# Linear attention inside a four-part network: prefix sums by scans along tokens, or by triangular matmuls with the token on the partition

## The chip, the cores and the metric

The kernel runs on one core of a Trainium2 chip. The metric is the device time of one execution in microseconds (us), taken as the median over runs. Before the change it is 2098.7 us (3 runs, 2096.18 to 2099.93). Everything is float32 in and out.

## What is computed

The input is 4 batches of 1024 tokens with 128 features. Four blocks follow each other, each with a layer norm and a residual: softmax attention, a top-2 mixture of 32 experts, linear attention, and the experts again. Only the linear attention is touched. It has 16 heads of 8 features; for each head:

```
qf = softplus(x @ Wq.T) * (sigmoid(x @ Wg.T + bg) + 1e-6)
kf = softplus(x @ Wk.T)
v  = x @ Wv.T
kv_cum = cumsum over tokens of kf[d] * v[e]        # 8 x 8 running sums
z_cum  = cumsum over tokens of kf[d]               # 8 running sums
num[e] = sum over d of qf[d] * kv_cum[d, e]
den    = sum over d of qf[d] * z_cum[d] + 1e-6
out    = (num / den) @ Wo.T
```

The running sums start again with each batch.

## The kernel before, in words

`network` runs the parts one after the other, each in a block of its own that ends with a barrier of all engines: load, `normalise`, `attention`, `normalise`, `experts`, `normalise`, `linear_attention` (L1096 to L1493), `normalise`, `experts`, `store`. `normalise` leaves the normalised input transposed, features on partitions, as a high part `k.xT_hi` and a rest `k.xT_lo`; a product in this split form takes three matmuls (`three`, L1416).

`linear_attention` works on 8 groups of 512 tokens. A tile has 128 partitions (16 heads times 8 features d) by 512 tokens; the second feature index e is unrolled into 8 columns, and column 0 stands for the denominator. For each group:

- TensorE makes gate, query and key (`projections`) and, for each e, v[e] spread over the d of its head (`v_column`, three matmuls each).
- ScalarE forms the gate and the logarithm of softplus (three table loads) and copies every second v column out of PSUM.
- The products k times v are split: odd e on VectorE (`kv`, L1334), even e on GpSimd (L1240).
- VectorE takes the running sum over the 512 tokens (`scan`, L1348), nine for each group, and does softplus, the reciprocal and the adding to x.
- GpSimd multiplies the nine running sums with the query (`product`, L1252).
- TensorE sums over d with a matrix of ones (`sum_over_d`, L1447 and L1452), then applies Wo (L1468).

Each engine has a hand-written order (`slot`) in which three groups overlap: `s` is projected, `s - 1` is summed, `s - 2` is finished. Counting semaphores tie the engines together; `pipeline` runs the middle slots in a loop over batches, where waits go through a register (`Rounds`), and SyncE fetches the input of each group into `xs_hi` and `xs_lo`. PSUM holds `z` (3 banks), `v_ps` (2), `num` (2) and `den_y` (1).

Of the kernel before, what the change touches and what calls it, by code (L numbers as in the profile page):

```python
# [7 lines left out]
ALU = mybir.AluOpType  # L8
# [1087 lines left out]
def linear_attention(nc, k, wq_dram, wk_dram, wv_dram, wo_dram, wg_dram, bg_dram):  # L1096

    HEADS, DH = 16, 8
    GATE_EPS, DEN_EPS = 1e-6, 1e-6
    HALVES = N // GT
    ROUNDS = B
    LEAD = 2
    COLS = DH + 1
    RING = 4  # L1110
    WEIGHTS = 5
    WQ, WK, WG, WV, WO = range(WEIGHTS)
    ZQ, ZK, ZG = (slice(n * GT, (n + 1) * GT) for n in range(3))

    SUM_ORDER = [1, 2, 3, 0, 4, 5, 6, 7, 8]
    SUM_AT = {j: n for n, j in enumerate(SUM_ORDER)}

    with ExitStack() as stack:
        s_ = Scope(nc, stack, "linear")
        sb, ps, sem = s_.sb, s_.ps, s_.sem  # L1120
        two = range(2)
        w = sb("w", [P, WEIGHTS, D])
        wT_hi, wT_lo = sb("wT_hi", [P, 3, D], F32R), sb("wT_lo", [P, 3, D], F32R)

        wv_hi, wv_lo = sb("wv_hi", [P, DH, HEADS, DH], F32R), sb("wv_lo", [P, DH, HEADS, DH], F32R)
        woT = sb("woT", [P, D])
        bg, ones = sb("bg", [P, 1]), sb("ones", [P, GT])
        same_head = sb("same_head", [P, HEADS, DH])
        into = sb("into", [P, DH, HEADS, DH])
        xs_hi = [sb(f"xs_hi{i}", [P, GT], F32R) for i in two]  # L1130
        xs_lo = [sb(f"xs_lo{i}", [P, GT], F32R) for i in two]
        log = sb("log", [P, 2 * GT])
        gate, soft_q = sb("gate", [P, GT]), sb("soft_q", [P, GT])
        q, kk = ([sb(f"{n}{i}", [P, GT]) for i in two] for n in ("q", "k"))
        v_col = [sb(f"v_col{i}", [P, GT]) for i in two]
        kv_dve, kv_pool = ([sb(f"{n}{i}", [P, GT]) for i in two] for n in ("kv_dve", "kv_pool"))
        cum = [[sb(f"cum{i}_{j}", [P, GT]) for j in range(COLS)] for i in two]
        prod0 = [sb(f"prod0_{i}", [P, GT]) for i in two]
        prod = [sb(f"prod{i}", [P, GT]) for i in range(RING)]
        den_inv, oT = ([sb(f"{n}{i}", [P, GT]) for i in two] for n in ("den_inv", "oT"))  # L1140
        z = ps("z", (P, 3 * GT))
        v_ps = [ps(f"v_ps{i}") for i in two]
        num = [ps(f"num{i}") for i in two]
        den_y = ps("den_y")

        w_in, bg_in, turned_ok, hi_ok, wT_ok, cleared, same_ok, const_ok = (sem(n) for n in (
            "w_in", "bg_in", "turned_ok", "hi_ok", "wT_ok", "cleared", "same_ok", "const_ok"))
        xs_in = [sem(f"xs_in{i}") for i in two]
        (z_ok, v_ok, v_out, kv_dve_ok, kv_pool_ok, cum_ok, prod_ok, sum_ok, gate_ok, log_step, soft_ok, q_ok,
         den_step, oT_ok, y_ok, x_ok) = (sem(n) for n in (  # L1150
             "z_ok", "v_ok", "v_out", "kv_dve_ok", "kv_pool_ok", "cum_ok", "prod_ok", "sum_ok", "gate_ok", "log_step",
             "soft_ok", "q_ok", "den_step", "oT_ok", "y_ok", "x_ok"))
        PER = {id(x): n * HALVES for x, n in (
            (z_ok, 1), (v_ok, DH), (v_out, 4), (kv_dve_ok, 4), (kv_pool_ok, 4), (cum_ok, COLS), (prod_ok, COLS),
            (sum_ok, COLS), (gate_ok, 1), (log_step, 3), (soft_ok, 2), (q_ok, 1), (den_step, 2), (oT_ok, 1), (y_ok, 1), (x_ok, 1))}

        def rounds(engine, *sems):
            scratch = engine.alloc_register(f"linear_value_{engine.engine.name}")
            return [Rounds(engine, x, PER[id(x)], scratch) for x in sems]

        def at(r, g, n=0):

            m = g * (r.per // HALVES) + n
            r.now(m) if m >= 0 else r.before(m + r.per)
# [395 lines left out]
```

## Time and profile before

| what | value |
|---|---|
| median of the runs | 2098.7 us |
| the profiled execution | 2101.55 us, its span 2099.6 us |
| TensorE busy | 1835.9 us (87%) |
| VectorE busy | 1683.0 us (80%) |
| GpSimd busy | 1346.3 us (64%) |
| ScalarE busy | 956.1 us (46%) |
| linear-attention stage | from 1590.2 to 1854.9 us of the span |
| mean granted TensorE clock, whole span | 0.941 |

The parts run one after the other, so an engine's share of the whole span is a mean over stages with different limits; the stage in question is read by itself. A granted clock of 1.0 is TensorE's 2.4 GHz, 0.5 its 1.2 GHz. The profiled execution took 2.9 us more than the median.

### The profile page before, as it was taken

To read this page: it belongs to the slowest core of one execution; us is meant where nothing else is said; L and a number is where in the kernel's file an instruction comes from. 1 tells how busy PE (TensorE), PEld (TensorE's weight loads), DVE (VectorE), ACT (ScalarE), POOL (GpSimd) and SP (SyncE) were. 2 spreads that over 40 slices of the span, in tenths; PEclk is the share of its full clock that TensorE was granted. 3 is DMA by queue.
4 is the path that set the end of the run, shared out by engine and by line. 5 is a ranking of instruction groups with operands and counts; after the bars stand their busy time and mean duration, and the time that the engine had idled before them with its cause. 6 is when DMAs were issued, how large, how long until landed. Compare 5 with 4: busy or idle time off the path is not lost. (4 is left out here: it accounts for less than half of the span.)

```text
span 2099.6 us, 35185 instructions
## 1 busy us (share of the span) xinstructions
PE 1835.9 (87%) x11743; PEld 1283.3 (61%) x11743; DVE 1683.0 (80%) x2683; ACT 956.1 (46%) x1920; POOL 1346.3 (64%) x1156
## 2 busy tenths in 40 slices
PE   2999999999999999999999998579974776666997
PEld 1666766666666666676666665458853333345885
DVE  4888888888888888888888886678874887967886
ACT  3344444444444444444444443347864323234885
POOL 2467657657667667667667668169972766714997
PEclk9999999999999999999999999589985989957998
DMA  2000000000000000000000000100000000000001
GB/s 81 1 1 1 2 1 1 1 1 2 1 1 1 1 1 1 1 1 1 1 1 1 2 1 1 41 31 21 30 0 26 21 20 19 2 1 31 21 30 40
DMA packets 22102, 23.20 MB, mean 11 GB/s; under 512 B 1296, under 2 KB 15440, under 8 KB 21968
## 3 DMA queue, kind: packets, MB, share of 16 engines
q1 hardware_dynamic: 21968, 21.40, 3.1%
q8 instruction: 85, 1.39, 0.3%
q14 instruction: 49, 0.40, 0.1%
HBM read 6.72 MB, written 2.10 MB: 4 GB/s over the span
## 5 line engine op out<-in xcount | busy, mean ns | idle before, releaser
L866 DVE TENSOR_REDUCE attn_neg<-attn_shared 128x2 f32<-128x1024 f32 x512 | 618.3, 1225 | 172.9 <-PE attn_shared L990 171.5
L806 ACT ACTIVATE attn_prob<-attn_shared 128x1024 f32<-128x1024 f32 (+3 forms) x384 | 311.0, 812 | 411.2 <-PE attn_shared L1018 411.2
L768 POOL TENSOR_TENSOR attn_row_sum<-attn_row_sum,attn_prob 128x1024 f32<-128x1024 f32 (+3 forms) x256 | 418.7, 1636 | 24.2
L481 ACT ACTIVATE experts_weighed<-experts_y,experts_gate 128x128 f32<-128x128 f32 x1024 | 278.1, 382 | 112.0 <-PE experts_y L570 108.6
L508 DVE SCALAR_TENSOR_TENSOR experts_acc<-experts_y,experts_gate,experts_acc 128x128 f32<-128x128 f32 x960 | 268.6, 344 | 43.4 <-PE experts_y L570 33.2
L763 POOL TENSOR_TENSOR attn_row_sum<-attn_prob 128x1024 f32<-128x1024 f32 x64 | 135.5, 2118 | 222.6 <-ACT attn_prob L806 220.1
L1035 PE MATMUL attn_pv<-attn_prob,attn_v 128*64 128x512 f32 (+3 forms) x1536 | 267.5, 490 | 1.2 <-POOL attn_prob L745 1.2
L568 PE MATMUL experts_y<-kept_w_hi,experts_xs_hi 128*128 128x512 f32 x512 | 201.2, 393 | 45.2 <-DMA experts_xs_lo<-kept_xT_lo 45.2
L986 PE MATMUL attn_shared<-attn_qk_hi 64*128 64x512 f32 x1024 | 223.0, 424 | 4.1 <-DVE attn_qk_lo L884 2.4
L890 DVE RECIPROCAL attn_den<-attn_den 128x256 f32<-128x256 f32 x128 | 214.6, 1718 | 12.1 <-ACT attn_den L829 12.1
L745 POOL TENSOR_TENSOR attn_prob<-attn_prob,attn_below 128x256 f32<-128x256 f32 x256 | 187.4, 732 | 49.6 <-ACT attn_prob L806 45.6
L990 PE MATMUL attn_shared<-attn_qk_hi,attn_qk_lo 64*128 64x512 f32 x1024 | 208.5, 392 | 0.0
L988 PE MATMUL attn_shared<-attn_qk_lo,attn_qk_hi 64*128 64x512 f32 x1024 | 207.6, 391 | 0.0
L1035 PEld LDWEIGHTS attn_pv<-attn_prob,attn_v 128*64 128x64 f32 x1536 | 104.4, 137 | 162.7 <-issue 148.8
L569 PE MATMUL experts_y<-kept_w_lo,experts_xs_hi 128*128 128x512 f32 x512 | 200.7, 392 | 0.0
L570 PE MATMUL experts_y<-kept_w_hi,experts_xs_lo 128*128 128x512 f32 x512 | 200.6, 392 | 0.0
L449 POOL TENSOR_TENSOR experts_quad_sum<-experts_quad_sum,experts_weighed 128x512 f32<-128x512 f32 x128 | 168.1, 1332 | 11.7 <-ACT experts_weighed L481 11.2
L775 POOL TENSOR_TENSOR attn_o_norm<-attn_o,attn_den 128x512 f32<-128x512 f32 x64 | 82.0, 1283 | 132.9 <-DVE attn_den L890 132.9
L986 PEld LDWEIGHTS attn_shared<-attn_qk_hi 64*128 64x128 f32 x1024 | 101.8, 184 | 90.7 <-issue 58.0
L1012 PE MATMUL attn_shared<-attn_qk_hi 64*128 64x512 f32 (+3 forms) x768 | 147.2, 374 | 9.8 <-DVE attn_neg L866 5.0
L1452 PE MATMUL linear_num<-linear_prod,linear_into 128*128 128x512 f32 x128 | 83.7, 748 | 67.7 <-POOL linear_prod L1252 67.6
L568 PEld LDWEIGHTS experts_y<-kept_w_hi,experts_xs_hi 128*128 128x128 f32 x512 | 97.2, 190 | 65.8 <-issue 45.4
(192 smaller groups left out, 3558.2 us busy)
## 6 DMA issues: line engine op xcount, KB each, us to landing
experts_xs_hi<-kept_xT_hi SPq DMA_DIRECT2D x16, 256.0 KB, 2.3
experts_xs_lo<-kept_xT_lo SPq DMA_DIRECT2D x16, 256.0 KB, 2.4
kept_x<-in_L_attn_a_x_dram SPq DMA_DIRECT2D x4, 512.0 KB, 6.2
norm_f_w_raw<-_ffn_expert_weights_dram SPq DMA_DIRECT2D x4, 512.0 KB, 6.1
linear_xs_hi<-kept_xT_hi SPq DMA_DIRECT2D x8, 256.0 KB, 2.3
linear_xs_lo<-kept_xT_lo SPq DMA_DIRECT2D x8, 256.0 KB, 2.4
out_dram<-kept_x SPq DMA_DIRECT2D x4, 512.0 KB, 5.4
attn_prob<-in_L_attn_a_Wkv_dram SPq DMA_DIRECT2D x2, 512.0 KB, 5.5
```

The source lines that it names most:

```text
L481: ins = act.activation(weighed[n][:, e, :], y[(2 * quad + odd) % BANKS][:, e * D:(e + 1) * D], ACT.Copy, scale=g)
L508: dve.scalar_tensor_tensor(out=acc[i][:, c, :], in0=y[(2 * quad + odd) % BANKS][:, e * D:(e + 1) * D], scalar=gate[i][:, c, quad * PER + e ...
L568: pe.matmul(out, xs_hi[i][:, at], hi, start=True, stop=False)
L569: pe.matmul(out, xs_hi[i][:, at], lo, start=False, stop=False)
L768: pool.tensor_tensor(row_sum[n][:, :, at:], row_sum[n][:, :, at:], src[:, :, at:], ALU.add).then_inc(add_ok, 1)
L806: act.activation(prob[n % RING][:, :, at:], buffer((p, i))[:, :, at:], ACT.Exp).then_inc(exp_ok, 1)
L866: dve.tensor_reduce(neg[p % 2][:, :, b, half], buffer((p, b, half))[:, :, :], AX.X, ALU.max, negate=True).then_inc(max_ok, 1)
L890: dve.reciprocal(den[n][:, at], den[n][:, at]).then_inc(inv_ok, 1)
L986: pe.matmul(buffer(u)[:, h, :], hi[head(h), 0, rows], hi[head(h), 1, at], start=True, stop=False)
L988: pe.matmul(buffer(u)[:, h, :], hi[head(h), 0, rows], lo[head(h), 1, at], start=False, stop=False)
L990: ins = pe.matmul(buffer(u)[:, h, :], lo[head(h), 0, rows], hi[head(h), 1, at], start=False, stop=True)
L1035: ins = pe.matmul(pv[head(h), first:], v[g % 2][:, j, cols], prob[(UNITS * p + i) % RING][:, h, first:], start=(j == 0), stop=(i in (7, 11)))
```

## The change

`linear_attention` is written anew; nothing else differs. Tokens now lie on the partitions, 128 (a chunk) at a time, four chunks to a group, 32 in all. The feature index d is innermost in memory.

- `project` makes gate, query, key and v of one chunk in one bank `z` of 512 columns: three matmuls of 512 columns, and one of 128 that adds the bias. ScalarE copies it out as `raw` (384 columns) and `v` (128, written into slots of nine, the ninth holds 1).
- `curves` (ScalarE) forms sigmoid and the logarithm of softplus for a whole group; `soften` (VectorE) ends softplus, `queries` (GpSimd) makes q.
- `outer` (GpSimd): the product k[d] times v[e], nine e by 128 columns: 1152 elements a chunk, into one of three `kv` buffers.
- `within` (TensorE): a matmul with the triangular matrix `upto` sums over the tokens of the chunk up to each, 3 pieces of 384 columns, into `cum` (3 banks, two of these).
- `carried` (TensorE): what the earlier chunks give, q transposed times `state`, 3 pieces of 48 columns, written into the ninth slot of each head. `add_state` keeps the sum over tokens in `state_ps`, and `new_state` (VectorE) masks it to each head's own.
- `weigh` (VectorE) multiplies the 1296 sums of a chunk with `q1` (q with a ninth slot that holds 1), and `add_up` sums nine neighbours. Then `floor` (ScalarE), `invert` (VectorE, 64 elements), `divide` (GpSimd), `turn_o` and `out` (TensorE), `into_x` (VectorE).
- `turn_q` transposes q for `carried`. `turn_q`, `project`, `turn_o` and `out` all use the one bank `z` in turn, and ScalarE or VectorE empties it each time.
- The eight groups are written out without a loop (`STEPS` is 11), and TensorE reads `k.xT_hi` and `k.xT_lo` in place; SyncE fetches only weights.

The core of the diff, with the order of ScalarE and VectorE:

```diff
+            def outer(g, c):
+                n = g * GROUP + c
+                pool.wait_ge(soft_ok, g + 1)
+                pool.wait_ge(v_ok, n + 1)
+                if n >= KV_RING:
+                    pool.wait_ge(cum_ok, n - KV_RING + 1)
+                pool.tensor_tensor(kv[n % KV_RING][:, :, :, :],
+                                   key(g, c).rearrange("p (h d) -> p h d", d=DH).unsqueeze(1).to_broadcast([P, E1, HEADS, DH]),
+                                   v[g % 3][:, c, :, :].rearrange("p h e -> p e h").unsqueeze(3).to_broadcast([P, E1, HEADS, DH]),
+                                   ALU.mult).then_inc(kv_ok, 1)
...
+                pool.tensor_tensor(o[:, :, :, :], num[g % 2][:, :, 0:DH, :].rearrange("p c e h -> p c h e"),
+                                   inv[:, :, :].unsqueeze(3).to_broadcast([P, GROUP, HEADS, DH]), ALU.mult).then_inc(o_ok, 1)
+
+            for s in range(STEPS):
+                g = s - 2
+                if exists(g):
+                    outer(g, 0)
+                    outer(g, 1)
+                if exists(g - 1):
+                    divide(g - 1)
+                if exists(g):
+                    outer(g, 2)
+                if exists(s - 1):
+                    queries(s - 1)
+                if exists(g):
+                    outer(g, 3)
...
+            def curves(g):
+                act.wait_ge(raw_ok, GROUP * (g + 1))
+                if g:
+                    act.wait_ge(soft_ok, g)
+                    act.wait_ge(q_ok, g)
...
+            def widen(g):
+                act.wait_ge(q_ok, g + 1)
...
+            for s in range(STEPS):
+                g = s - 2
+                if exists(g):
+                    q_out(g)
+                    widen(g)
+                if exists(s):
+                    projected(s, 0)
+                if exists(g - 1):
+                    floor(g - 1)
+                if exists(s):
+                    for c in range(1, GROUP):
+                        projected(s, c)
+                if exists(g - 1):
+                    o_out(g - 1)
+                if exists(s):
+                    curves(s)
...
-                    start = cum[0][j][:, GT - 1:GT] if i else 0.0
-                    dve.tensor_tensor_scan(cum[i][j][:, :], ones[:, :], src[:, :], start,
-                                           ALU.mult, ALU.add).then_inc(cum_ok, 1)
...
+            for s in range(STEPS):
+                g = s - 2
+                for c in range(GROUP):
+                    if exists(g):
+                        n = g * GROUP + c
+                        weigh(g, c)
+                        if not begins(n + 1):
+                            new_state(n + 1)
+                        add_up(g, c)
+                    if c == 0 and exists(g - 1):
+                        invert(g - 1)
+                    if c == 1 and exists(s - 1):
+                        soften(s - 1)
+                    if c == 2 and exists(g - 1):
+                        into_x(g - 1)
...
+            def within(g, c):
+                n = g * GROUP + c
+                pe.wait_ge(kv_ok, n + 1)
+                if n >= 2:
+                    pe.wait_ge(prod_ok, n - 1)
```

How the order moves, first on ScalarE in a middle slot. Before, the gate, the logarithm's steps and the copies of v columns are interleaved:

```order
L333 REGISTER_ALU [waits linear_z_ok]
L1295 ACTIVATE linear_gate<-linear_z,linear_bg 128x512 [waits linear_q_ok]
L333 REGISTER_ALU [waits linear_v_ok]
L1289 ACTIVATE linear_v_col<-linear_v_ps 128x512 [waits linear_kv_pool_ok]
L1299 ACTIVATE linear_log<-linear_z 128x1024 [waits linear_soft_ok]
L1301 ACTIVATE linear_log<-linear_log 128x1024 [waits linear_log_step]
```

After, from the end of one step (`linear_oT` is the copy of `turn_o`) into the next (`linear_qT` is the copy of `turn_q`):

```order
L1284 ACTIVATE linear_oT<-linear_z 128x512 [waits linear_o_turned]
L1257 ACT_TABLE_LOAD [waits linear_q_ok,linear_soft_ok]
L1257 ACTIVATE linear_gate<-linear_raw 128x512 [waits linear_raw_ok]
L1259 ACTIVATE linear_gate<-linear_gate 128x512 [waits linear_gate_step]
L1260 ACTIVATE linear_log<-linear_raw 128x1024
L1262 ACTIVATE linear_log<-linear_log 128x1024 [waits linear_log_step]
L1264 ACTIVATE linear_log<-linear_log,linear_upto 128x1024 [waits linear_log_step]
L1274 ACTIVATE linear_qT<-linear_z 128x512 [waits linear_q_turned]
L1270 ACTIVATE linear_q_1<-linear_q 128x64x8 [waits linear_prod_ok,linear_q_ok]
L1245 ACTIVATE linear_raw<-linear_z 128x384 [waits linear_soft_ok,linear_z_ok]
```

The whole of `curves` stands in one piece between the last copy of a step and the first of the next. Two of its three table loads are not printed in this form.

On TensorE, before, around the sum for the denominator:

```order
L1452 MATMUL linear_num<-linear_prod,linear_into 128x512
L333 REGISTER_ALU x2
L1447 MATMUL linear_den_y<-linear_prod_1,linear_same_head 128x512
L333 REGISTER_ALU
L1417 MATMUL linear_v_ps<-linear_xs_hi,linear_wv_hi 128x512
L1418 MATMUL linear_v_ps<-linear_xs_lo,linear_wv_hi 128x512
L1419 MATMUL linear_v_ps<-linear_xs_hi,linear_wv_lo 128x512
```

After, from the third chunk of a group into the next step:

```order
L1415 MATMUL linear_cum<-linear_kv,linear_upto 128x48x8 x3
L1398 MATMUL linear_z<-kept_ident,linear_o 128x128 x4
L1426 MATMUL linear_cum<-linear_state,linear_qT 128x48 x3
L1435 MATMUL linear_state_ps<-linear_v,linear_soft 128x144
L1405 MATMUL linear_z<-linear_woT,linear_oT 128x128 x4
L1415 MATMUL linear_cum<-linear_kv,linear_upto 128x48x8 x3
L1426 MATMUL linear_cum<-linear_state,linear_qT 128x48 x3
L1435 MATMUL linear_state_ps<-linear_v,linear_soft 128x144
L1392 MATMUL linear_z<-kept_ident,linear_q 128x128 x4
L1415 MATMUL linear_cum<-linear_kv,linear_upto 128x48x8 x3
L1384 MATMUL linear_z<-linear_wT_hi,kept_xT_hi 128x512
```

`turn_o` (L1398) now stands behind `within` of the third chunk, and `project` (L1384) of the next group behind the transposes of q (L1392), whose copy it waits for.

## Rows read from the trace of the kernel before

**Rows 1.** Windows, the stage: us; busy PE, PEld, DVE, ACT, POOL; PEclk; DMA, GB/s.
```profile
1590.20:1854.90 264.70, 174.18 (x477) 96.22 (x477) 201.45 (x162) 81.15 (x91) 167.88 (x117) 0.84 0.05 17
```
**Rows 2.** Timeline, first projection and last operation of the stage: start us, us, engine.
```profile
1599.50 0.76 PE L1417 MATMUL linear_z<-linear_xs_hi,linear_wT_hi 128*128 128x512 f32 x1 [4.30 <-DVE linear_wv_lo L1318]
...
1854.19 0.69 DVE L1369 TENSOR_TENSOR kept_x<-linear_den_y,kept_x 128x512 f32<-128x512 f32 x1 [1.25 <-PE linear_den_y L1468]
```
**Rows 3.** Waits of the stage: who waits, for whom; us in total, times, longest.
```profile
PE linear_num L1452 <- POOL linear_prod L1252: 67.6, 35, 4.5
...
DVE linear_den_inv L1377 <- PE linear_den_y L1447: 21.4, 7, 5.0
```
**Rows 4.** Timeline, VectorE's reciprocals of two neighbouring groups.
```profile
1729.76 3.32 DVE L1398 RECIPROCAL linear_den_inv<-linear_den_inv 128x512 f32<-128x512 f32 x1
...
1760.60 3.32 DVE L1398 RECIPROCAL linear_den_inv<-linear_den_inv 128x512 f32<-128x512 f32 x1
```
**Rows 5.** Groups by shape, VectorE (count, busy us, mean ns of one).
```profile
L866 DVE TENSOR_REDUCE attn_neg<-attn_shared 128x2 f32<-128x1024 f32 x512 | 618.3, 1225 | 172.9 <-PE attn_shared L990 171.5
...
L890 DVE RECIPROCAL attn_den<-attn_den 128x256 f32<-128x256 f32 x128 | 214.6, 1718 | 12.1 <-ACT attn_den L829 12.1
...
L884 DVE TENSOR_TENSOR attn_qk_lo<-attn_shared,attn_qk_hi 128x1024 fp32r<-128x1024 f32 x64 | 73.7, 1189 | 7.7 <-POOL kept_x L738 7.0 <-ACT attn_qk_hi L810 0.7
...
L1348 DVE TENSOR_TENSOR_SCAN linear_cum<-linear_ones,linear_cum,linear_kv_pool 128x512 f32<-128x512 f32 x16 | 28.2, 1761 | 1.1 <-POOL linear_kv_pool L1240 1.1
...
L1398 DVE RECIPROCAL linear_den_inv<-linear_den_inv 128x512 f32<-128x512 f32 x8 | 26.6, 3321 | 0.0
...
L1334 DVE TENSOR_TENSOR linear_kv_dve<-linear_v_ps,linear_k 128x512 f32<-128x512 f32 x32 | 21.3, 667 | 19.7 <-PE linear_v_ps L1419 19.4
...
L1393 DVE SCALAR_TENSOR_TENSOR linear_q<-linear_gate,linear_soft_q 128x512 f32<-128x512 f32 x8 | 13.0, 1629 | 0.1
```
**Rows 6.** Groups by shape, GpSimd.
```profile
L768 POOL TENSOR_TENSOR attn_row_sum<-attn_row_sum,attn_prob 128x1024 f32<-128x1024 f32 x96 | 229.3, 2388 | 11.7
...
L1252 POOL TENSOR_TENSOR linear_prod<-linear_q,linear_cum 128x512 f32<-128x512 f32 x72 | 116.8, 1641 | 24.1 <-DVE linear_cum L1348 21.6 <-PE linear_num L1452 2.5
...
L768 POOL TENSOR_TENSOR attn_row_sum<-attn_row_sum,attn_prob 128x512 f32<-128x512 f32 x64 | 82.5, 1289 | 5.0
```
**Rows 7.** Groups by shape, ScalarE.
```profile
L806 ACT ACTIVATE attn_prob<-attn_shared 128x256 f32<-128x256 f32 x64 | 24.6, 385 | 46.1 <-PE attn_shared L1018 46.1
...
L1289 ACT ACTIVATE linear_v_col<-linear_v_ps 128x512 f32<-128x512 f32 x32 | 19.0, 595 | 119.2 <-PE linear_v_ps L1419 119.2
...
L1301 ACT ACT_TABLE_LOAD x8 | 10.3, 1283 | 0.1
...
L1305 ACT ACTIVATE linear_log<-linear_log,linear_ones 128x1024 f32<-128x1024 f32 x8 | 9.2, 1149 | 0.1
...
L1301 ACT ACTIVATE linear_log<-linear_log 128x1024 f32<-128x1024 f32 x8 | 8.5, 1057 | 0.1
...
L1295 ACT ACTIVATE linear_gate<-linear_z,linear_bg 128x512 f32<-128x512 f32 x8 | 5.5, 687 | 7.3 <-PE linear_z L1419 7.3
```
**Rows 8.** Timeline, TensorE matmuls in the middle of the stage.
```profile
1727.14 2.08 PE L1452 MATMUL linear_num<-linear_prod,linear_into 128*128 128x512 f32 x2 [2.38 <-POOL linear_prod L1252]
...
1734.09 0.40 PE L1418 MATMUL linear_z<-linear_xs_lo,linear_wT_hi 128*128 128x512 f32 x1
...
1734.32 0.39 PE L1419 MATMUL linear_z<-linear_xs_hi,linear_wT_lo 128*128 128x512 f32 x1
...
1737.66 1.15 PE L1468 MATMUL linear_den_y<-linear_woT,linear_oT 128*128 128x128 f32 x8 [0.85 <-DVE linear_oT L1360]
...
1742.02 1.12 PE L1452 MATMUL linear_num<-linear_prod,linear_into 128*128 128x512 f32 x2 [2.51 <-POOL linear_prod L1252]
...
1748.58 2.07 PE L1452 MATMUL linear_num<-linear_prod,linear_into 128*128 128x512 f32 x2 [3.18 <-POOL linear_prod L1252]
```
**Rows 9.** Granted clock, one stretch of the stage, columns as in rows 1.
```profile
1749.00:1753.00 4.00, 4.00 (x6) 1.73 (x6) 0.52 (x1) 0.00 (x0) 0.74 (x1) 0.50 0.00 0
```

More of the change, by code:

```diff
@@ L1128, in linear_attention @@
[L1128 to L1147, printed above, removed]
@@ L1184, in exists @@
-        def exists(g, r):
-            return g >= 0 and not (isinstance(r, int) and r == ROUNDS - 1 and g >= HALVES)
-        block = s_.block()
+        bg_raw, bg = sb("bg_raw", [P, D]), sb("bg", [P, D], F32R)
+        pick_raw, pick = sb("pick_raw", [P, P]), sb("pick", [P, P], F32R)
+        upto, own = sb("upto", [P, P]), sb("own", [P, HEADS])
+        raw = [sb(f"raw{i}", [P, GROUP, 3 * D]) for i in two]
+        v = [sb(f"v{i}", [P, GROUP, HEADS, E1]) for i in three]
+        log = sb("log", [P, GROUP, 2 * D])
@@ new lines, in invert, with into_x, soften @@
+            def invert(g):
+                dve.wait_ge(den_ok, g + 1)
+                if g:
+                    dve.wait_ge(o_ok, g)
+                dve.reciprocal(inv[:, :, :], den[:, :, :]).then_inc(inv_ok, 1)
+            def into_x(g):
+                x = k.x[:, g * GROUP:(g + 1) * GROUP, :]
+                dve.wait_ge(y_ok, g + 1)
+                dve.tensor_tensor(x, z[:, :].rearrange("p (c d) -> p c d", d=D), x, ALU.add).then_inc(x_ok, 1)
+            def soften(g):
+                dve.wait_ge(log_step, 3 * (g + 1))
+                if g >= 2:
+                    dve.wait_ge(kv_ok, GROUP * (g - 1))
+                    dve.wait_ge(q_ok, g - 1)
+                    dve.wait_ge(added_ok, updates(GROUP * (g - 1)))
+                dve.scalar_tensor_tensor(out=soft[g % 2][:, :, :], in0=raw[g % 2][:, :, D:3 * D], scalar=0.0, in1=log[:, :, :],
+                                         op0=ALU.max, op1=ALU.add).then_inc(soft_ok, 1)
@@ new lines, in turn_q, with turn_o @@
+            def turn_q(g):
+                pe.wait_ge(q_ok, g + 1)
+                for c in range(GROUP):
+                    ins = pe.transpose(z[:, c * P:(c + 1) * P], q[:, c, :], k.ident[:, :])
+                ins.then_inc(q_turned, 1)
+            def turn_o(g):
+                pe.wait_ge(o_ok, g + 1)
+                for c in range(GROUP):
+                    ins = pe.transpose(z[:, c * P:(c + 1) * P], o[:, c, :, :].rearrange("p h e -> p (h e)"), k.ident[:, :])
+                ins.then_inc(o_turned, 1)
@@ new lines, in carried @@
+            def carried(g, c):
+                n = g * GROUP + c
+                m = updates(n)
+                pe.wait_ge(qT_ok, g + 1)
+                if not begins(n):
+                    pe.wait_ge(state_ok, m)
+                held = empty if begins(n) else state[m % 2]
+                for b in range(3):
+                    to = sums(n)[:, b, :, :].rearrange("p e (h d) -> p e h d", d=E1)[:, :, :, DH]
+                    ins = pe.matmul(to, qT[g % 2][:, c * P:(c + 1) * P], held[:, 3 * b:3 * b + 3, :], start=True, stop=True)
+                ins.then_inc(cum_ok, 1)
```

520 lines of the change are left out of this document (218 added, 302 removed).

## The prediction

> **What bounds the kernel now.** The parts of the network run one after the other with a barrier between them, and the diff touches only the linear attention, so I read that stage alone. First the windows view over 1590.2 to 1854.9 us [rows 1]: in 264.7 us VectorE is busy 201.5, TensorE 174.2, GpSimd 167.9 and ScalarE 81.2, and the granted clock is 0.84. No engine is full: the stage is a ring of waits. The waits view [rows 3] shows two links: TensorE waits 67.6 us for GpSimd's products, and VectorE 21.4 us for the denominator that TensorE sums from them, 5.0 us at the longest. The timeline [rows 4] gives the period: reciprocals of neighbouring groups start at 1729.76 and 1760.60, so a group costs 30.8 us. Of this VectorE works 201.5 / 8 = 25.2 us [rows 1], mostly nine scans of about 1.76 us and a reciprocal of 3.32 [rows 5]. So the old limit is VectorE's work plus one round trip over GpSimd and TensorE, eight times, and a start: 9.3 us pass up to the first projection [rows 2].
>
> **What is removed.** For each group nine scans (15.8 us), the reciprocal over 512 columns (3.32) and four products of k and v on VectorE (2.7) [rows 5]; nine products and four of k and v on GpSimd, thirteen operations of 512 columns, 21 us by 167.9 / 8 [rows 1]; 24 matmuls for v columns on TensorE. Also the eight fetches of xs from the resident input: no wait for them is among the rows, I cost them at nothing.
>
> **What is added, engine by engine and group.** I price by width, along rows of the same kind.
>
> - VectorE: an operation with one operand in PSUM takes 0.667 us for 512 columns and 1.189 for 1024 [rows 5], so 1.02 ns a column: `weigh` (1296) 1.47, `new_state` (144) 0.29. A reduction takes 1.225 for 1024, so `add_up` (1296) 1.50. The reciprocal is 1.718 for 256 and 3.321 for 512, so 64 columns cost 0.52. `soften` is 1.19 undisturbed, 3.3 if it suffers like the query product (1.629 for 512). `into_x` 0.67. Sum 4 x 3.26 + 0.52 + 1.19 + 0.67 = 15.4 us.
> - GpSimd: 1.289 for 512 columns, 2.388 for 1024 [rows 6], so `outer` (1152) is 2.66; four of them, `queries` and `divide` at 1.29 each: 13.2 us.
> - ScalarE [rows 7]: `curves` is three table loads (3.85), sigmoid 0.69, its copy 0.60, absolute value and exponential 1.06 each, logarithm 1.15, together 8.4. Copies: 0.60 for 512, 0.385 for 256, so 0.49 and 0.28 for `raw` and `v`. With `q_out`, `widen`, `o_out` and `floor`: 13.6 us.
> - TensorE at full clock [rows 8]: a matmul of the split form and 512 columns starts 0.23 us after the last (1734.09, 1734.32) and ends 0.17 later than it would stream. A plain float32 product is two instructions: 1.12 for the pair at 512 columns, 0.17 of it the end, so about 0.92, and 384 columns cost 0.69. Eight instructions of 128 columns take 1.15, so 0.12 each. So: `project` 0.82, `within` 3 x 0.69 = 2.07, `carried` six short instructions 0.73, `add_state` 0.27, `turn_q` and `turn_o` 0.5 each, `out` 0.98. Sum 4 x 3.89 + 2.0 = 17.5 us. I have no row for a transpose at full clock and took 0.12; at 0.24 each a turn is 1.0.
>
> No engine reaches 20 us, against 30.8. What decides is the ring.
>
> **The new ring.** `curves` of group s stands in one piece on ScalarE ahead of `q_out` of the next step, as the order rows show, and all projections queue on bank z behind `q_out`. Following the waits through one step:
>
> `curves` 8.4; `q_out` 0.6; `project` and `carried` of the first chunk 0.82 + 0.73 + 0.17; `weigh` 1.47; `new_state` 0.29; `add_up` 1.50; `invert` 0.52 (it stands behind `add_up`); `divide` 1.29; third `outer` 2.66 (behind `divide` on GpSimd); third `within` 2.07; `turn_o` with its end 0.67 (behind that `within`); `o_out` 0.6; then `curves` again. Sum 21.8 us. The handovers (about 0.06 each) are paid for by operations of VectorE and ScalarE that start before the last has ended.
>
> Beside it lies this: `soften` follows the second `add_up`, `queries` and the fourth `outer` follow `soften`; the last `add_up` comes out some 2 us ahead of the `floor` that needs it. That cover of 2 us is all: if the third `outer` holds `soften` back for longer, this branch ends last. The second `within` and projections 2 to 4 fill TensorE's waits.
>
> The ring holds 4.1 us of TensorE at full clock. Here the clock does not stay full: after 2.38 us idle the pair took 2.08, after 2.51 us 1.12, after 3.18 us 2.07 [rows 8], and such a stretch shows 0.50 in the windows [rows 9]. The new step has idle times of about 1.7 and 2.3 us, so some of them may be followed by half clock. I take the stage's mean of 0.84: 4.1 / 0.84 = 4.9, and the step is 22.6 us.
>
> **Two readings of GpSimd.** On the same 512 columns GpSimd took 1.641 in the old stage and 1.289 in the attention [rows 6], and VectorE's scan 1.76. Of the new operations of VectorE only `soften` has both tensors in SBUF, so I price GpSimd undisturbed. At 1641 / 1289 = 1.27 for all, `outer` would be 3.39 and `divide` 1.64, the step 1.1 us longer, the total 7 to 8 us more. The Trainium skill, SBUF — State Buffer, Who interferes with whom, says that a VectorE instruction with two SBUF inputs contends with a GpSimd instruction that reads SBUF and that one with a single SBUF input does not. The trace agrees as far as rows go: 1.641 beside the scans, 1.289 without. By the rule the sum is the one that I use.
>
> **The whole stage.** Lead: 9.3 us less the two 1024-wide splits of v's weights (about 2.2) is 7.1 to the first `project`. Then four chunks at half clock, each `project` 1.7, ends 0.2, copies 0.77: 10.4. `curves` of group 0, 8.4. Four chunks of group 1, the first projected already: 8.6. `curves` of group 1, 8.4. That is 42.9 us in which nothing overlaps. Then six steps with a `curves` in the ring: 6 x 22.6 = 135.6. Group 6 has no projections: about 20 us to its last `add_up`; group 7 about 18; its finish (`floor` 0.3, `invert` 0.52, `divide` 1.29, `turn_o` 0.67, copy 0.6, `out` 1.15, `into_x` 0.67) 5.2; with 1.5 for the clock 45. Sum 223.5 us against 264.7, a gain of 41.2. Against the profiled execution, 2101.6 us, that gives 2060.4; this lies 2.9 us above the median shown, so against 2098.7 the forecast is 2057.5, in round figures 2058. The median is told from no change beyond about 0.2%, 4.2 us.
>
> **Rivals.**
>
> - *GpSimd's strided reads cost more.* `outer` repeats v across eight neighbours and walks it with a step of nine elements; `divide` reads `num` with a step of 16. All of rows 6 run over neighbours, so no row speaks for or against it. At the dearest pace among them, 1.641 us for 512 or 3.2 ns a column, `outer` is 3.7 and `divide` 1.64: the ring grows by 1.0 + 0.35 to 24.0, while GpSimd's own 17.7 us stay below it. `soften` waits longer behind the third `outer`, and the branch with the fourth closes in. With 1.4 us over six steps, 3 over the last two and some 3 for that branch it is 2072. The Trainium skill, GPSIMD Engine Reference, Performance pitfalls for Q7 kernels, gives about 50% more for reads with a step above 8 bytes; by it, as an estimate, `outer` would be 4.0 and the total about 2076; no run here shows it yet. Chance 0.24.
> - *TensorE stays at half clock (the other side).* At 0.5 the group needs 35 us of TensorE, more than the old period, and the loop becomes TensorE's own queue: 36 us a step with what cannot be filled. From 1.2 GHz throughout: 43 + 6 x 36 + 80 = 339 us, 74 more than now, 2173. The turning point is where 43 + 6 T + 45 = 264.7, a step of 29.4 us. For it: stretches at 0.50 exist [rows 9]. Against: they follow idle times of 2.4 us and more in a stage where TensorE is busy for 66% of it [rows 1]; here 17.5 / 22.6 = 77%. Only a clock near half all the time, or half clock with the dearer GpSimd, passes the point. Chance 0.10.
> - *The ring does not close as I drew it.* If `curves` is cheaper or the clock stays full, the step is 21 to 21.8 and the total 2042 to 2052. Chance 0.14, counted as its own below 2046.
> - *The change does not do what it says.* The v columns and scans are gone from the order rows, so the work has changed; a stage that comes out equal by chance: 0.02.
>
> **How the numbers follow.** My own case (2046 to 2066) has 0.50, dearer GpSimd 0.24, cheaper 0.14, half clock 0.10, equal 0.02. The predicted time is that of the likeliest, 2058. The range takes in the clock at full (2042, and 4 below for narrow operations that I may price too high) and dearer GpSimd with `soften` at 3.3 and the clock at 0.75 (2072 + 14): 2038 to 2086, which leaves out the slow end. Faster by over 0.2%: 0.88; within: 0.02; slower: 0.10.
>
> **What would show it.** Right: the stage is about 223 us; `inv` reciprocals of neighbouring groups lie 22 to 23 us apart; ScalarE's idle time before `linear_oT` ends on TensorE; the third `within` waits for GpSimd; GpSimd's 1152-wide product near 2.7 us; VectorE's 1296-wide pair near 1.5 each. Wrong: `outer` at 4 us; TensorE's granted clock below 0.75 over the stage; VectorE without idle time; or a step above 25 us.

## The result, and the profile after

The changed kernel takes 2066.5 us (median of 4 runs, 2065.55 to 2068.0) against 2099.3 beside it: a ratio of 0.984, 95% interval 0.983 to 0.986. The gain is 32.8 us, where 41.2 were forecast (2058). The profiled execution has a span of 2064.6 us. Outside the linear attention nothing moved: it begins at 1589.9 (before: 1590.2), and from its end to the end of the span there are 245 us in both traces.

Windows view of the changed kernel. Columns: stretch, its us; busy us of PE, PEld, DVE, ACT, POOL; PEclk; DMA share, GB/s. First the stage, then its lead (the time up to the first step) and the six steps that have a `curves` in them; the end, 49.7 us, is not printed. A step runs from one `linear_qT` copy of ScalarE to the next.

```profile
1589.90:1819.40 229.50, 169.56 (x701) 121.55 (x701) 118.47 (x119) 102.84 (x164) 97.23 (x61) 0.80 0.01 2
...
1589.90:1631.10 41.20, 20.23 (x47) 12.84 (x47) 2.48 (x4) 22.98 (x37) 10.18 (x16) 0.54 0.03 8
1631.10:1655.30 24.20, 19.46 (x71) 14.72 (x72) 11.43 (x11) 11.97 (x19) 8.25 (x4) 0.72 0.00 1
1655.30:1677.70 22.40, 18.66 (x93) 13.36 (x91) 16.74 (x17) 12.65 (x20) 11.94 (x6) 1.00 0.00 1
1677.70:1699.10 21.40, 17.29 (x88) 12.77 (x88) 14.72 (x15) 12.69 (x22) 11.92 (x6) 1.00 0.00 0
1699.10:1722.10 23.00, 18.59 (x86) 13.27 (x86) 14.60 (x14) 12.60 (x21) 11.92 (x6) 0.93 0.00 1
1722.10:1746.30 24.20, 20.80 (x86) 15.49 (x87) 12.99 (x14) 12.66 (x22) 11.91 (x6) 0.79 0.00 1
1746.30:1769.40 23.10, 19.35 (x90) 13.83 (x88) 16.23 (x17) 12.62 (x21) 11.95 (x6) 0.93 0.01 1
```

Read this against [rows 1]: 229.5 us instead of 264.7, VectorE busy 118.5 instead of 201.5, GpSimd 97.2 instead of 167.9, TensorE 169.6 against 174.2. That is the whole gain of about 35 us in the trace (span 2099.6 to 2064.6). The period, 30.8 us before [rows 4], is 21.4 us where the granted clock is 1.00 throughout, and 24.2 where it is 0.79 and 0.72. The step of 22.4 us ran at 1.00 as well, but began with a leftover of the slow one before it: the last `within` of that step ended at 1657.25, 1.9 us after the copy of q had begun, and held back the first projection.

Groups by shape of the changed kernel (count, busy us, mean ns of one, idle time before them):

```profile
L1324 DVE TENSOR_TENSOR linear_prod<-linear_cum,linear_q 128x1296 f32<-128x1296 f32 x32 | 48.2, 1506 | 81.2 <-PE linear_cum L1426 81.1
L1333 DVE TENSOR_REDUCE linear_num<-linear_prod 128x144 f32<-128x1296 f32 x32 | 47.8, 1494 | 0.1
L1352 DVE SCALAR_TENSOR_TENSOR linear_soft<-linear_raw,linear_log 128x1024 f32<-128x1024 f32 x8 | 9.7, 1217 | 18.6 <-ACT linear_log L1264 18.6
L1339 DVE RECIPROCAL linear_inv<-linear_den 128x64 f32<-128x64 f32 x8 | 4.4, 545 | 0.3 <-ACT linear_den L1280 0.3
...
L1194 POOL TENSOR_TENSOR linear_kv<-linear_soft,linear_v 128x1152 f32<-128x1152 f32 x32 | 75.3, 2374 | 0.0
L1212 POOL TENSOR_TENSOR linear_o<-linear_num,linear_inv 128x512 f32<-128x512 f32 x8 | 10.6, 1320 | 70.5 <-DVE linear_inv L1339 70.5
```

These answer to [rows 5, 6]: no scan, no wide reciprocal; the pair of 1296 costs 1.51 and 1.49 us, the outer product 2.37.

Waits of the changed kernel's stage (who, for whom: us in all, times, longest):

```profile
DVE linear_prod L1324 <- PE linear_cum L1426: 81.1, 25, 18.8
...
ACT linear_oT L1284 <- PE linear_z L1398: 48.8, 8, 12.8
...
PE linear_cum L1415 <- POOL linear_kv L1194: 22.6, 10, 4.3
```

TensorE waits 22.6 us for GpSimd, where it waited 67.6 [rows 3]; VectorE now waits 81.1 us and ScalarE 48.8 for TensorE. The ring closes as drawn: `divide` at 1683.80, the third outer behind it, TensorE behind that, `oT` behind `turn_o`, then the next table load. Timeline of the changed kernel in the step with full clock (start us, us, engine; the projections and the other chunks left out):

```profile
1683.80 1.32 POOL L1212 TENSOR_TENSOR linear_o<-linear_num,linear_inv 128x512 f32<-128x512 f32 x1 [7.87 <-DVE linear_inv L1339]
...
1685.08 2.37 POOL L1194 TENSOR_TENSOR linear_kv<-linear_soft,linear_v 128x1152 f32<-128x1152 f32 x1
...
1687.51 2.20 PE L1415 MATMUL linear_cum<-linear_kv,linear_upto 128*128 128x384 f32 x6 [1.85 <-POOL linear_kv L1194]
...
1689.04 1.26 POOL L1205 TENSOR_TENSOR linear_q<-linear_gate,linear_soft 128x512 f32<-128x512 f32 x1 [1.59 <-issue]
...
1690.18 0.60 ACT L1284 ACTIVATE linear_oT<-linear_z 128x512 f32<-128x512 f32 x1 [3.83 <-PE linear_z L1398]
...
1690.80 1.28 ACT L1257 ACT_TABLE_LOAD   x1
```

Look at the fourth row too. `queries` ended at 1690.30, and `curves`, which writes the same `gate` tile again, could not begin before that. It began at 1690.80: a second ring of waits, from `curves` through the second `add_up`, `soften` and `queries` back to `curves`, stands 0.5 us behind the first. In the step of 1722.1 it was the later one:

```profile
1736.65 1.27 POOL L1205 TENSOR_TENSOR linear_q<-linear_gate,linear_soft 128x512 f32<-128x512 f32 x1 [3.74 <-PE linear_cum L1426]
...
1738.02 1.28 ACT L1257 ACT_TABLE_LOAD   x1 [1.69 <-POOL linear_q L1205]
```

### The profile page after: what moved, and what is told of

It reads as the page before. It is cut to its first block and busy times, and to the rows that moved or that the text cites. A ratio compares the mean times of both kernels' runs of the same rounds, so it can differ in the third digit from the quotient of the medians.

```text
span 2064.6 us, 35025 instructions
## 1 busy us (share of the span) xinstructions
PE 1831.8 (89%) x11967; PEld 1310.0 (63%) x11967; DVE 1599.8 (77%) x2640; ACT 977.6 (47%) x1993; POOL 1275.7 (62%) x1099
## 5 line engine op out<-in xcount | busy, mean ns | idle before, releaser
L768 POOL TENSOR_TENSOR attn_row_sum<-attn_row_sum,attn_prob 128x1024 f32<-128x1024 f32 (+3 forms) x256 | 418.7, 1636 | 24.2
L763 POOL TENSOR_TENSOR attn_row_sum<-attn_prob 128x1024 f32<-128x1024 f32 x64 | 135.6, 2119 | 222.5 <-ACT attn_prob L806 220.0
L1016 PE MATMUL attn_shared<-attn_qk_hi,attn_qk_lo 64*128 64x512 f32 (+3 forms) x768 | 135.5, 343 | 0.0
```

Source lines behind the costliest of these rows:

```text
L768: pool.tensor_tensor(row_sum[n][:, :, at:], row_sum[n][:, :, at:], src[:, :, at:], ALU.add).then_inc(add_ok, 1)
```

## The experiments

The kernel before was run beside each batch of them (its medians 2098.8 to 2100.6). The table gives the median, and from each trace the lead (up to the first `linear_qT`), the six steps, and the end (groups 6 and 7 and the finish), in us. The trace is of one execution: for "changed, filled" it took 2058.2 us and for "two SBUF inputs" 2077.7, the slowest of their runs. One row shows how far a small gap can be trusted. "One SBUF input" is the changed kernel with more work and nothing taken away, and came out 3.8 us faster; in its trace the fifth step is one of 21.4 us at full clock, where the changed kernel has 24.2. So between kernels whose clock varies, a gap of 3 or 4 us alone proves nothing of the edit.

| kernel | median (range) | lead | six steps | end |
|---|---|---|---|---|
| changed | 2066.5 (2065.6 to 2068.0) | 41.2 | 24.3, 22.4, 21.4, 23.0, 24.2, 23.1 | 49.7 |
| outers first | 2060.7 (2060.3 to 2061.2) | 41.8 | 23.9 six times | 39.1 |
| gate twice | 2063.6 (2061.9 to 2067.8) | 40.7 | 24.2, 22.4, 22.5, 21.4, 23.7, 21.9 | 48.9 |
| both | 2040.7 (2040.3 to 2041.7) | 41.8 | 20.0, 19.3, 20.8, 22.5, 19.3, 22.5 | 37.8 |
| longer curves | 2072.3 (2071.6 to 2073.8) | 42.1 | 25.2, 24.0, 24.5, 23.5, 22.7, 25.0 | 48.1 |
| changed, filled | 2055.5 (2052.6 to 2058.2) | 42.5 | 24.6, 23.8, 21.4 four times | 45.7 |
| both, filled | 2028.9 (2028.5 to 2030.5) | 41.1 | 17.0, 20.4, 19.3 four times | 37.0 |
| two SBUF inputs | 2072.9 (2071.1 to 2077.7) | 42.8 | 24.0, 23.1, 24.4, 22.8, 24.8, 23.3 | 54.5 |
| one SBUF input | 2062.7 (2061.9 to 2064.8) | 42.1 | 24.6, 22.4, 21.4, 23.0, 21.4, 23.1 | 51.0 |
| split | 2021.1 (2020.4 to 2023.2) | 40.3 | 19.7, 17.4 five times | 36.6 |
| split, filled | 2017.9 (2016.5 to 2018.8) | 42.0 | 17.0, 17.4 five times | 35.2 |
| split, lead filled | 2014.8 (2013.6 to 2015.8) | 34.8 | 20.3, 17.4 five times | 35.2 |
| split, all filled | 2012.2 (2011.7 to 2012.9) | 36.1 | 17.0, 17.4 five times | 35.2 |

**One ring or two.** The edits, alone and together.

Outers first:

```diff
-                    outer(g, 0)
-                    outer(g, 1)
+                    for c in range(GROUP):
+                        outer(g, c)
                 if exists(g - 1):
                     divide(g - 1)
-                if exists(g):
-                    outer(g, 2)
                 if exists(s - 1):
                     queries(s - 1)
-                if exists(g):
-                    outer(g, 3)
```

> All four outer products go ahead of divide and queries on GpSimd. Theory 1 (the ring as the prediction draws it is the only one): the third within no longer waits for divide and the third outer, it starts when the fourth projection ends, 1.85 us earlier in the step of 1677.7 to 1699.1. Steps at full clock 19.5 us, over six steps 11 us, and the 2.6 and 4.3 us waits of the last two groups go: 2066.5 - 11 - 5 = 2050. Theory 2 (a second ring of nearly the same length stands behind it: curves waits for queries of the group before, since gate is one buffer; queries ended 1690.3 and curves began 1690.8, so 0.5 us of cover): steps at full clock 20.9 to 21.1, 2 to 3 us over six steps, and only the last two groups gain in full: 2058. On either theory the fourth within no longer waits for GpSimd.

Gate twice (the wait for `soften` moves behind the gate part with it; `queries` reads `gate[g % 2]`):

```diff
-        gate = sb("gate", [P, GROUP, D])
+        gate = [sb(f"gate{i}", [P, GROUP, D]) for i in two]
...
-                if g:
-                    act.wait_ge(soft_ok, g)
-                    act.wait_ge(q_ok, g)
+                if g >= 2:
+                    act.wait_ge(q_ok, g - 1)
...
+                if g:
+                    act.wait_ge(soft_ok, g)
                 act.activation(log[:, :, :], raw[g % 2][:, :, D:3 * D], ACT.Abs).then_inc(log_step, 1)
```

> gate is held twice, so that curves does not wait for queries of the group before; GpSimd's order is as in the changed kernel. Theory 1 (only the drawn ring counts): nothing, 2066.5. Theory 2 (a second ring through gate, 0.5 us shorter than the first): nothing in the steps at full clock either, since the first ring still holds 21.4 us, but up to 2 us where curves waited for queries (5.7 us of such waits in the changed kernel): 2064.5 to 2066.5.

Both:

> Both edits together: the outers first, and gate twice. Theory 1: as with the outers alone, 2050, since gate was never in the way. Theory 2: now both rings are cut; the step is about 19.8 us at full clock, 1.6 less than 21.4, ten over six steps, 2 in the lead (curves of group 1 need not wait), and the 7 of the last two groups: 2047, 10 below the outers alone. A gain of this run over the outers alone that is larger than that of the gate alone over the changed kernel speaks for two rings.

Measured: 5.8 us less with the outers first, 2.9 less with the gate twice, 25.8 less with both. The 2.9 can't be told from nothing: the ratio to the kernel before is 0.982 to 0.986, that of the changed kernel 0.983 to 0.986. Apart they give at most 8.7; that both give three times as much is what two rings of almost equal length do. By stage: the six steps took 5.0 us more with the outers first, 2.3 less with the gate twice, 13.9 less with both; the end 10.6, 0.8 and 12.0 less. With one ring the outers alone were expected at 2050. The clock does not explain the gain of both: with TensorE's waits filled (below), steps at full clock take 21.4 us in the changed kernel and 19.3 with both, and the medians differ by 26.6. The single edits were not run filled. Waits of the kernel with the outers first, 1655 to 1775 us, show the second ring in the open:

```profile
ACT L1253 <- POOL linear_q L1205: 8.5, 5, 1.7
...
PE linear_z L1380 <- ACT linear_qT L1270: 20.8, 5, 4.4
```

`curves` waits for `queries` in each of five steps, 1.7 us, and TensorE then idles 4 us ahead of the next projection. Its clock falls (0.86 in each of these steps), so the steps are 23.9 us and not the 21 I expected: from the first projection to the end of the second `within` it is 7.7 us (1703.94 to 1711.64), against 4.8 in the changed kernel's step of 1699.1, and these 2.9 us are the difference. The gain of this edit lies in the end alone, 39.1 instead of 49.7, where no `curves` stands. The second ring decides between the theories. The sizes were off both ways: 2060.7 for 2058 with the outers alone, by the clock, and 2040.7 for 2047 with both, where steps and end shrank by more than expected (13.9 for 10 and 12.0 for 7).

**Is curves in the ring?**

```diff
+                act.activation(spare[:, :, :], raw[g % 2][:, :, D:3 * D], ACT.Abs)
                 act.activation(log[:, :, :], raw[g % 2][:, :, D:3 * D], ACT.Abs).then_inc(log_step, 1)
```

> The changed kernel with one operation more in curves on ScalarE: the absolute value is also written to a spare tile, 1.04 us. Theory 1 and 2 (curves lies in the ring): the step grows one to one, 22.4 us at full clock, and both curves of the lead too: 8 x 1.04 = 8.3 us, 2075. Rival (the step is set by another engine's queue or by TensorE's clock, and ScalarE has room: it is busy 12.7 of 21.4 us): less than 3 us, below 2069.5.

Measured 5.8 us more. Over the six steps it is 144.9 instead of 138.3 us, 1.1 for each added 1.04, and the one step at full clock takes 22.7 instead of 21.4 or 22.4; the lead grew by 0.9 and the end came out 1.6 shorter. So ScalarE, busy for 12.7 of 21.4 us, is in the ring with `curves`. That it counts one to one is not shown so closely, since by the clock the same sum came to 135.7 in the run with one SBUF input. The end, which has no `curves`, moves by more than a microsecond from kernel to kernel with the clock.

**Is the missing term the clock?** Matmuls into sums that are written over anyway, placed in TensorE's waits:

```diff
+            def keep_busy(n, times):
+                pe.wait_ge(prod_ok, n - 1)
+                for _ in range(times):
+                    pe.matmul(cum[n % 2][:, 0, :], pick[:, :], wT_hi[:, :], start=True, stop=True)
...
                     within(g, 0)
+                    keep_busy(g * GROUP + 1, 6)
...
+                    keep_busy(g * GROUP + 2, 7 if g < GROUPS - 1 else 18)
                     within(g, 2)
...
+                    if not exists(g):
+                        keep_busy(g * GROUP, 20)
                     turn_o(g - 1)
```

> The changed kernel with matmuls of 512 columns whose result is written over, in TensorE's waits: 6 ahead of the first projection of a step, 7 ahead of the third within (18 in the last group), 20 ahead of the last turn_o. Theory (the term missed in the forecast is the clock after idle time): all steps come to the 21.4 us seen at full clock, 128.4 for six instead of 138.3, and the last part loses two within at half clock (4 us), and 1.5 in turn_o and out: about 15 less, 2051. Rival 1 (the clock falls whatever TensorE does, or the slow steps are slow for another reason): no gain, 2066. Rival 2 (the added matmuls hold up the ones that count more than the clock gives back): over 2066.

Measured 2055.5, 11 less, with TensorE doing more work (8.1 less between the two profiled executions). Windows of this kernel, columns as above:

```profile
1702.19:1723.56 21.37, 20.33 (x102) 14.87 (x100) 14.60 (x14) 12.65 (x22) 11.95 (x6) 1.00 0.00 1
1723.56:1744.95 21.39, 20.09 (x101) 15.09 (x101) 14.72 (x15) 12.64 (x21) 11.97 (x6) 1.00 0.00 0
...
1784.88:1812.08 27.20, 24.83 (x122) 18.51 (x120) 16.99 (x18) 2.82 (x6) 7.39 (x4) 1.00 0.00 1
```

The last four steps are all 21.4 us with the clock at 1.00, and the end is 45.7 instead of 49.7. The first step, which comes out of the slow lead, stayed slow (24.6), and the second, 23.8 at full clock, is 1.4 longer than in the changed kernel. There the filling itself was in the way: the last `within` of the slow step and the six matmuls behind it ended at 1660.3, and the first projection began 3.1 us after the copy of q, not 0.6. On top of both, 8 such matmuls ahead of the first projection of a step and 20 ahead of the last `turn_o`:

> Both (outers first, gate twice) with 8 matmuls whose result is written over ahead of the first projection of each step and 20 ahead of the last turn_o. Theory (clock): the steps of 20.8, 22.5 and 22.5 us come down to 19.3 to 19.8: about 7 less, 1.5 in the finish, 2032. Rival: the step is not set by TensorE's pace, the slow ones stay: 2040.

Measured 2028.9, 11.8 less than both alone, more than the 9 expected. The first step went from 20.0 to 17.0, the last four are 19.3 each.

**VectorE beside GpSimd.** One more VectorE operation after the third `add_up`, while GpSimd makes outer products: once with two inputs in SBUF, once with one.

```diff
+                    if c == 2 and exists(g):
+                        dve.tensor_tensor(spare[:, :, :], soft[g % 2][:, :, :], soft[g % 2][:, :, :], ALU.mult)
```

> The changed kernel with one VectorE product of 1024 columns more in each group, both inputs in SBUF, after the third add_up, when GpSimd works on the outers of the next group. Two questions. Off the ring or on it: the last add_up was 2.6 us ahead of the floor that needs it, so an operation of 1.1 us costs nothing (2066.5) and one of 3.3 about 0.7 a step (2071); if VectorE's work lay on the ring, 1.1 to 3.3 a step, 2073 to 2086. Contention: if an instruction of VectorE with two SBUF inputs disturbs GpSimd, the product takes about 2 to 3.3 us and the outer product beside it more than 2.37, up to 3.4; if not, 1.1 and 2.37.

```diff
+                    if c == 2 and exists(g):
+                        dve.tensor_reduce(spare[:, :, :], soft[g % 2][:, :, :].rearrange("p c (h d) -> p c h d", d=DH), AX.X, ALU.add)
```

> The counterpart of the run with a product of two SBUF inputs: in the same place of VectorE's order a reduction of 1024 columns with one input in SBUF. Theory (two SBUF inputs are what suffers beside GpSimd, and VectorE's branch has 2.6 us of cover): it takes 1.22 us although GpSimd's outers run beside it, and the time stays 2066.5 within 2. Rival (any VectorE operation that reads SBUF suffers beside GpSimd): 2.8 us and 2073, as there. Rival 2 (VectorE lies on the ring): 1.2 a step, 2075.

Measured 2072.9 with two inputs and 2062.7 with one. The spare operation took 1.21 us each of eight times with one input (minimum, median, maximum: 1207, 1207, 1210 ns). With two it took 1217, 2776, 3129 ns. Timeline of that kernel; GpSimd's three outer products in a row come as one line:

```profile
1648.32 8.02 POOL L1195 TENSOR_TENSOR linear_kv<-linear_soft,linear_v 128x1152 f32<-128x1152 f32 x3
...
1693.68 7.04 POOL L1195 TENSOR_TENSOR linear_kv<-linear_soft,linear_v 128x1152 f32<-128x1152 f32 x3
```

And the added product in the same trace:

```profile
1649.91 1.85 DVE L1370 TENSOR_TENSOR linear_spare<-linear_soft 128x1024 f32<-128x1024 f32 x1
...
1699.03 2.78 DVE L1370 TENSOR_TENSOR linear_spare<-linear_soft 128x1024 f32<-128x1024 f32 x1
...
1817.88 1.22 DVE L1370 TENSOR_TENSOR linear_spare<-linear_soft 128x1024 f32<-128x1024 f32 x1
```

Three outers of 7.04 us are 2.35 each, so the one running at 1699.03 ended at 1700.7. The product stood for those 1.7 us and then took 1.1. Where it began in the first of three (1649.91), it waited for 0.8 us, and the next outer was held up in turn: 8.02 instead of 7.04. Alone, at 1817.88, it takes 1.22. So the two do not slow each other, they take turns by whole instructions. The Trainium skill, SBUF — State Buffer, Summary: rules for kernel authors, says that, of a VectorE operation with two SBUF inputs and a GpSimd operation that reads SBUF, the second to issue "fully blocks" until the first finishes; these rows agree. The two added operations differ in kind too, a product and a reduction, so the number of inputs is not the only difference between them. But the kernel before shows turns with a third kind, VectorE's scans of two SBUF inputs:

```profile
1708.82 3.41 POOL L1252 TENSOR_TENSOR linear_prod<-linear_q,linear_cum 128x512 f32<-128x512 f32 x2
...
1711.04 2.27 DVE L1348 TENSOR_TENSOR_SCAN linear_cum<-linear_ones,linear_cum,linear_kv_dve 128x512 f32<-128x512 f32 x1
```

The first line is two products in a row, of 2.19 and 1.26 us. Of all 72 products 39 took 1.26 to 1.30 us, 7 about 1.71 and 26 about 2.18; the scans took 1.19 to 2.29. The mean of 1.641 in [rows 6] is a mixture of products that had to stand and products that did not, and no product's own pace.

The operation with one input cost nothing that can be seen: the steps at full clock are 21.4 us as before, as VectorE's branch has 2.6 us of cover. The 2.78 us one used that up and cost 6.4 (two more than I expected, steps and end both at a lower clock).

**The next limit.** With both rings cut, `o_out` goes between the gate part of `curves` and its logarithm part:

```diff
                     for c in range(1, GROUP):
                         projected(s, c)
+                if exists(s):
+                    curves(s)
                 if exists(g - 1):
                     o_out(g - 1)
                 if exists(s):
-                    curves(s)
+                    logs(s)
```

> On top of both (outers first, gate twice), o_out stands between the gate part and the logarithm part of curves on ScalarE, so that curves does not wait for turn_o. Theory: the ring through divide, turn_o and o_out is now 3 us shorter, the step at full clock falls from the 19.3 of both to about 18, near TensorE's own 17.5; little idle time is left and the clock stays full: 6 x 18 = 108 instead of 124.4, total 2040.7 - 16 = 2025. Rival (at this density the clock falls nevertheless, or the wait moves to queries, which curves no longer hides): 2032 or more.

Measured 2021.1, 19.6 less than both. A step of it:

```profile
1684.68:1702.09 17.41, 16.91 (x89) 12.57 (x87) 14.59 (x15) 12.54 (x22) 12.01 (x7) 1.00 0.00 1
```

TensorE is busy 16.9 of 17.4 us and keeps its clock by itself. What is left idles in the lead and at the end, so these were filled too. First 12 matmuls behind the first `within` of all and 20 ahead of the last `turn_o`:

> The version with outers first, gate twice and curves split, and with matmuls whose result is written over in the two places where its TensorE still idles for long: 12 behind the first within of group 0, 20 ahead of the last turn_o. Theory (clock after idle time): its first step comes down from 19.7 to about 17.4 us, the last turn_o and out from 1.1 and 2.1 to 0.6 and 1.1: 3.8 less than the 2021.1 of the split alone, 2017. Rival (the cold first step is due to the start of the pipeline, not to the clock): 2020 or more.

Then the lead as well, in part ahead of the first weights (`early` is a matmul of `xT_hi` with itself into `cum[1]`; not all places are shown):

```diff
+            early(12)
             pe.wait_ge(w_in, 16 * WEIGHTS)
...
                     project(s, 0)
+                    if s < 2:
+                        early(28 if s else 2)
```

> As the one before, and the lead is filled too: 12 such matmuls ahead of the wait for the weights, 4 ahead of the split weights, 2 behind each projection of groups 0 and 1 and 28 behind the first of group 1, 16 behind the first within. In the lead every projection takes 1.7 us at half clock and lies with ScalarE's copies in one chain; seven of them lie on it. Theory: 0.8 us less each, 5 us, so 2012. Rival (the added matmuls are in the way as much as they help, or the lead hangs on ScalarE alone): 2017 or more.

Measured 2017.9 and 2014.8. Filled, the lead fell from 42.0 to 34.8, but the first step rose from 17.0 to 20.3: 16 matmuls end 2.62 us ahead of the step's first projection. Timeline of the kernel with the lead filled:

```profile
1618.57 4.12 PE L1449 MATMUL linear_cum<-linear_wT_hi,linear_pick 128*128 128x512 f32 x16
1625.30 0.51 PE L1391 MATMUL linear_z<-linear_wT_hi,kept_xT_hi 128*128 128x512 f32 x1 [2.62 <-ACT linear_qT L1273]
...
1628.10 0.80 PE L1391 MATMUL linear_z<-linear_wT_hi,kept_xT_hi 128*128 128x512 f32 x1
```

With 26 of them:

> As the filled lead before, with 26 instead of 16 matmuls behind the first within. There TensorE was still idle for 2.62 us ahead of the first step, which then ran at a clock of 0.83 and took 20.25 us, where the same step took 17.01 in the run with 12 of them after a slow lead. Theory (the clock follows the idle time): no idle time over 0.5 us is left there, the step takes 17.0: 3.2 less than 2014.8, 2011.5. Rival (TensorE cannot be held at full clock that long, or the matmuls run past the wait): 2014 or more.

Measured 2012.2 us, ratio 0.958 (0.956 to 0.960) to the kernel before, 54 us faster than the changed kernel. The first step is 17.0 again, with a lead of 36.1.

## Why the prediction was right, and what it missed

- **The old limit and the ring.** The new ring was right. At full clock the forecast is 21.8 us and the measured step 21.4; the waits stand in the order drawn, and 1.04 us added to `curves` came back as 1.1. The old limit is a reading of the trace before; no run changed the old kernel to test it.
- **The prices.** Right to 0.05 us on VectorE: 1.51, 0.30, 1.49, 0.55, 1.22. `outer` was 2.37 and not 2.66. `within` was 2.10 to 2.20 (2.07), `carried` 0.76 to 0.82 (0.73), a turn 0.60 to 0.62 with its end (0.67). The `outer` that was priced too dear explains most of the 0.4 us between the two rings.
- **The rival of GpSimd's strided reads.** It fell: `outer` costs 2.06 ns a column where neighbours cost 2.33 [rows 6], `divide` with a step of 16 elements (64 bytes) 1.320 us against 1.289. The Trainium skill, GPSIMD Engine Reference, Performance pitfalls for Q7 kernels, has about 50% more for reads with a step above 8 bytes. `divide`, whose innermost step is that large, doesn't show it; `outer` is a weaker case, as its innermost step is that of a repeated or a neighbouring element.
- **GpSimd undisturbed.** Right: none of the 32 outers was slower than 2.40 us. The runs with one and with two SBUF inputs show why: the new VectorE work reads PSUM or one tile of SBUF. The exception, `soften`, took 1.21 to 1.23 us each time and never stood beside a GpSimd operation, so its dearer price of 3.3 was not put to the test. The two readings set 1.641 against 1.289 as two paces; the trace of before has one pace, 1.26 to 1.30, and turns (above), so the dearest price that the rival took, 3.2 ns a column, was a mixed mean.
- **The lead.** 41.2 against 42.9: shorter by 1.7. (Its four chunks of 1.7, 0.2 and 0.77 add up to 10.7 and not 10.4.)
- **The clock: the mis-sized term.** "I take the stage's mean of 0.84" was applied to 4.1 us of TensorE in the ring, and 1.5 us to the end. The stage had 0.80, and slow stretches do not spread evenly: a third `within` that follows its wait at half clock takes 4.21 instead of 2.20. The six steps took 138.3 against 135.6, the end 49.7 against 45: group 6 ended its last `add_up` after 22.2 us (20), group 7 20.5 later (18), the finish took 7.0 (5.2). 2.7 and 4.7 less the 1.7 of the lead is the 5.7 us by which the stage of 229.2 exceeds the forecast 223.5.
- **How much of it was clock.** With the waits filled the steps and the end took 8.4 us less (133.9 and 45.7), against 6.3 that the forecast had allowed for the clock in them (0.8 a step, 1.5 at the end). The filled kernel still has a first step of 24.6 out of the slow lead, 3.2 above the later ones. So most of the missing microseconds were clock, but not all are accounted for: its end of 45.7, nearly at full clock, is 2.2 above the forecast's 43.5 without the clock.
- **Luck in the total.** A ring priced 0.4 too long (2.4 over six steps) and the lead's 1.7 paid for part of the slow steps, which cost 9.9 us over 6 x 21.4, where 4.8 had been allowed. The traces differ by 35.0 us and the medians by 32.8, since the profiled execution of before lies 2.2 us above its median (2101.55 against 2099.3).
- **Not seen: the second ring.** The prediction priced a branch through `soften`, `queries` and the fourth outer with 2 us of cover. The one that mattered runs through `queries` and back to `curves` by way of the single `gate` tile, with 0.5 us of cover. It cost the changed kernel little by itself (two waits, 5.7 us in all, 4.1 of them in the first of the six steps, which took 24.2 with the gate held twice as well), so the forecast stands. For the next edit it matters: from the drawn ring alone the outers first were expected at 2050, and 2060.7 came.
- **The half-clock rival.** Its mechanism is real in single steps (0.72, 0.79), but no step came near its turning point of 29.4 us; the longest was 24.3.

Left open: why the steps of one kernel fall into 21.4, 23.0 and 24.2 us, though their order is the same. The clock rises where idle time is filled, but why a wait of 1.85 us sometimes brought half clock and sometimes not was not tried.

## What to carry to other kernels

When work is in a ring of waits, look for the second-longest ring before shortening the first: a buffer that is written again closes one too. Cutting either alone gave 6 us and something too small to tell, both together 26. Price TensorE's part of a ring at either clock level and at the place where it follows a wait, not at a stage's mean; matmuls whose result nobody reads, put into those waits, gave 11 us here, but can get in the way where a step is late already. Before crediting an edit with 3 or 4 us, look whether the steps only fell otherwise between the two clock levels. A VectorE operation with two SBUF inputs takes turns with GpSimd by whole instructions, so give it one input in PSUM, as `weigh` has (1.51 us, the outers beside it undisturbed), or put it where GpSimd idles, as `soften` does.

## What the runs showed of the hardware

- TensorE's granted clock fell to 0.50 after idle times of 1.85 us (the third `within` of the step of 1699.1 took 3.69 us; the windows have 0.50 from 1709.6 to 1711.6) and 2.61 us (4.21 us), and stayed at 1.00 after another wait of 1.85 us in the step before (2.20 us).
- Four transposes of 128 columns take 0.60 us at full clock and 1.06 to 1.12 at half, and the split kernel, in which TensorE is busy for 97% of a step (16.9 of 17.4 us) with eight of them in it, keeps 1.00.
- A GpSimd product with an operand repeated over eight neighbours is no dearer than one that walks over neighbours, 2.06 against 2.33 ns a column; one that reads with a step of 16 elements took 1.320 us for 512 columns against 1.265 for `queries`.
- Contention between VectorE and GpSimd is no slower pace but a turn: 1.7 us of standing and 1.1 of work, as worked out above. It goes both ways: three outers took 8.02 us instead of 7.04.
